# Second input tile sooner, later ones scaled by ScalarE; next MLP weights decoded mid-stage and split in the first half of stage four

## The reference, cut to what matters

```python
xn = layernorm(x)                                  # x: 8 x 256 tokens x 256
x  = x + attn(xn) + ffn(xn)
# attn, 16 heads of 128: q, k (with rope), v, g = xn @ W.T
#   s  = clip(xn @ Ws1.T @ Ws2.T + bs2, -32, 32)   # 64 slots a head
#   z  = cumlogsumexp(s); es = exp(s); enz = exp(-z)
#   A  = tril(q @ k.T) * scale
#   qv = softmax(enz * (A @ es))
#   o  = tril((qv * enz) @ es.T) @ v
#   out = (rmsnorm(o) * g_norm * silu(g)) @ Wo.T
# ffn: gate, up (2048 wide), down from 4-bit codes times scales per block of 32
#   out = (gelu(gate) * up) @ down.T
```

## Time and profile before

| | us |
|---|---|
| median of 3 runs | 1124.58 (1122.58 to 1124.82) |
| the profiled execution | 1122.49 |
| its span, first to last instruction | 1120.0 |
| TensorE busy | 1084.0 (97%) |
| VectorE busy | 928.1 (83%) |
| ScalarE busy | 650.6 (58%) |
| GpSimd busy | 425.5 (38%) |

### The profile page before, as it was taken

One profiled execution on the slowest core, in us unless ns is written; L12 is line 12 of the kernel. 1 busy time (PEld: TensorE's weight loads), 2 busy tenths in 40 slices (PEclk: granted clock), 3 DMA queues, 4 the chain that ended last, 5 costly groups with the idle time before them and its releaser, 6 DMA issues.

```text
span 1120.0 us, 20624 instructions
## 1 busy us (share of the span) xinstructions
PE 1084.0 (97%) x7176; PEld 927.7 (83%) x7176; DVE 928.1 (83%) x1687; ACT 650.6 (58%) x2103; POOL 425.5 (38%) x308
## 2 busy tenths in 40 slices
PE   6888999999999999999999999999999999999996
PEld 5677888888888888888888888888888888888875
DVE  6788889888888889888888888888888898888863
ACT  4465566655655657555666656565665556655542
POOL 7142245432524345232453324443252334523231
PEclk9899999999999999999999999999999999999996
DMA  4002000020002000020000200011000200000001
GB/s 166 1 1 78 1 2 1 2 77 1 1 1 78 1 2 1 1 78 1 1 1 1 78 1 2 1 38 41 1 1 1 78 1 1 1 1 20 1 20 38
DMA packets 9526, 23.06 MB, mean 21 GB/s; under 512 B 848, under 2 KB 5840, under 8 KB 8528
## 3 DMA queue, kind: packets, MB, share of 16 engines
q1 hardware_dynamic: 9424, 21.76, 5.4%
HBM read 19.66 MB, written 2.10 MB: 19 GB/s over the span
## 4 chain that ended last, share of the span: by engine, by line
PE 84%; DVE 7%; issue 4%; POOL 2%; ACT 2%; DMA 0%; POOLq 0%; DVEq 0%; ACTq 0%
PE bank L205 20%; PE bank L207 19%; PE bank L206 19%; PE bank L303 4%; PE bank L366 4%; PE bank L316 3%; PE bank L337 3%; DVE xs L930 2%; PE bank L375 2%; PE bank L305 2%; PE bank L328 1%; PE bank L529 1%; PE bank L346 1%; PE bank L319 1%; PE bank L359 1%
## 5 line engine op out<-in xcount | busy, mean ns | idle before, releaser
L1200 POOL TENSOR_TENSOR inter_lo<-ffb,inter_hi 128x512 fp32r<-128x512 f32 x64 | 83.3, 1325 | 440.5 <-ACT inter_hi L678 440.5
L1191 POOL TENSOR_TENSOR qkT<-ra,xs 128x512 f32<-128x512 f32 x128 | 170.2, 1329 | 109.6 <-DVE xs L930 80.8
L640 ACT ACTIVATE sm<-bank,mx 128x64 f32<-128x64 f32 x256 | 76.5, 326 | 120.6 <-DVE mx L886 120.6
L930 DVE TENSOR_TENSOR xs<-xs,rope 128x512 f32<-128x512 f32 x128 | 129.5, 1012 | 0.0
L927 DVE TENSOR_TENSOR ra<-bank,rope 128x512 f32<-128x512 f32 x128 | 87.7, 685 | 46.9 <-ACT xs L622 44.7
L621 ACT ACTIVATE xs<-bank 64x512 f32<-64x512 f32 x128 | 76.2, 595 | 66.8 <-PE bank L207 43.8
L205 PE MATMUL bank<-xh,wqk_hi 128*128 128x512 f32 x256 | 109.9, 429 | 3.1 <-DVE h L990 2.6
L875 DVE RECIPROCAL enzT<-enzT 128x256 f32<-128x256 f32 x64 | 111.4, 1742 | 0.0
L205 PE MATMUL bank<-xh,wgu_hi 128*128 128x512 f32 x256 | 105.6, 412 | 0.0
L645 ACT ACTIVATE At<-bank 128x128 f32<-128x128 f32 x128 | 35.8, 281 | 114.1 <-DVE At L809 112.9
L205 PE MATMUL bank<-wvg_hi,xh 128*128 128x512 f32 x256 | 101.1, 395 | 1.0 <-DVE xl L978 1.0
(11 more groups left out here) (149 smaller groups left out, 3075.5 us busy)
## 6 DMA issues: line engine op xcount, KB each, us to landing
raw<-in_w_qkvg SPq DMA_DIRECT2D x7, 1024.0 KB, 5.0
scaled<-in_w_scaled SPq DMA_DIRECT2D x8, 640.0 KB, 7.1
packed<-in_w_packed SPq DMA_DIRECT2D x8, 384.0 KB, 5.7
acc<-in_x SPq DMA_DIRECT2D x4, 512.0 KB, 8.1
out<-acc SPq DMA_DIRECT2D x3, 512.0 KB, 2.9
raw<-in_w_qkvg SPq DMA_DIRECT2D x2, 512.0 KB, 7.1
out<-acc SPq DMA_DIRECT2D x2, 256.0 KB, 2.1
ws_raw<-in_w_slot SPq DMA_DIRECT2D x8, 48.0 KB, 1.8
```

The lines of the kernel that those rows point to most:

```text
L640: ins = act.activation(sm[:, c], src[:, c], ACT.Exp, bias=mx[:, g:g + 1], accum_out=ssum[:, g:g + 1])
L930: dve.tensor_tensor(two(xs[i % 2][:, :]), two(xs[i % 2][:, :]), sin, ALU.mult).then_inc(sin_done, 1)
L1191: pool.tensor_tensor(qkT[:, i, :], ra[i % 2][:, :], xs[i % 2][:, :], ALU.add).then_inc(roped, 1)
L1200: pool.tensor_tensor(inter[1][e][:, :], ffb[e][:, :], inter[0][e][:, :].bitcast(F32), ALU.subtract).then_inc(inter_lo, 1)
```

## The change

SyncE: x 1 is loaded fourth, ahead of `ws1`, `packed`, `ws2_raw`, `scaled`; of the next head pair `packed` is loaded first. The layer norm has buffers of its own (`xvar`, `xrs`, `xnb`) in place of `mse` and `rstd`. x 2 and x 3 are no longer scaled by VectorE but by ScalarE, which needs a bias of -mean times scale that VectorE makes (`x_bias`). On the way in, VectorE does the statistics of x 1 at once, scales x 1 between the decode steps, and takes the first gates in between too; both transposes of x 1 follow each other; `slot_scores(None, 0, 0)` and `slot_inner(1)` stand ahead of stage 0, and the statistics of x 2 too. In stages 0 and 1 the first transposes of the next x come after `outputs` and `project_vg`.

For every head pair: `decode` of the next one runs in the middle of stage two (steps 0, 1) and three (steps 2, 3, 4); before, steps 1 and 3 stood at stage ends and step 4 in stage four. `prepare_scales` moves to stage three, `prepare_out` to stage one of its own head pair. In stage four the high and low parts of VG, QK and GU are all made before `softmax_exp`.

`wqk_hi` now stands between the two `off_diagonal` copies (At), where before it came after `copy_state`. The core of the diff:

```diff
@@ SyncE
             load_x(0)
...
+            load_x(1)
             sp.dma_start(ws1, w_slot1).then_inc(ws1_in, 16)
...
-            load_x(1)
@@ TensorE
             project_qk(0, 0, 0, 1)
             transpose_x(1, 0, rg[1])
+            transpose_x(1, 1, sc[0])
             project_qk(0, 0, 0, 2)
             project_qk(0, 0, 0, 3)
+            pe.wait_ge(h1_done, 2)
+            pe.wait_ge(h1_lo, 1)
+            slot_scores(None, 0, 0)
+            slot_inner(1, sc[1])
...
                 for i in (0, 1):
+                    if first and i == 1:
+                        pe.wait_ge(h1_done, 4)
+                        pe.wait_ge(h1_lo, 2)
...
+                if not first:
+                    outputs(st, 0, php, None)
+                if not last:
+                    project_vg(st + 1, nbp, nhp, 2, True)
                 if prep:
                     pe.wait_ge(clip_done, st + 2)
                     transpose_x(prep, 0, sc[0])
-                if not first:
-                    outputs(st, 0, php, None)
-                if not last:
-                    project_vg(st + 1, nbp, nhp, 2, True)
                 slot_rows(st)
@@ ScalarE
+            def x_scale_act(bp):
+                act.wait_ge(xnb_done, bp - 1)
+                if bp == 3:
+                    act.wait_ge(xT_full, KT * bp)
+                for i in range(NT):
+                    ins = act.activation(xn[bp][:, i, :], acc[:, bp * NT + i, :], ACT.Identity,
+                                         bias=xnb[:, i:i + 1], scale=xrs[:, i:i + 1])
+                ins.then_inc(xn_act, 1)
...
+                if bp == 0 and not first:
+                    prepare_out(hp)
+                if bp == 2 and more:
+                    prepare_scales(hp + 1)
                 if bp == 3 and more:
                     split_hi(hp + 1, W_VG)
                 off_diagonal(st, 2)
+                if bp == 3 and more:
+                    split_hi(hp + 1, W_QK)
                 off_diagonal(st, 3)
                 gate_square(st, 1)
+                if first:
+                    x_scale_act(prep)
...
                 copy_state(st)
+                if bp == 3 and more:
+                    split_hi(hp + 1, W_GU)
+                if st == 1:
+                    x_scale_act(prep)
@@ VectorE
+            def x_bias(bp):
+                dve.wait_ge(xpow_done, bp + 1)
+                wait(dve, xn_act, bp - 2)
+                dve.scalar_tensor_tensor(out=xnb[:, :], in0=mv[:, :, 0], scalar=-1.0, in1=xrs[:, :],
+                                         op0=ALU.mult, op1=ALU.mult).then_inc(xnb_done, 1)
...
+                softmax_in(st, par)
+                if first:
                     cumulate(1, 1)
-                softmax_in(st, par)
...
+                if bp == 2 and more:
+                    decode(hp + 1, 2)
+                    decode(hp + 1, 3)
                 softmax_max(st)
...
                     add_share(st, pbp, 0)
+                if bp == 1 and more:
+                    decode(hp + 1, 0)
+                    decode(hp + 1, 1)
                 if bp == 2 and more:
-                    decode(hp + 1, 2)
-                if bp == 3 and more:
                     decode(hp + 1, 4)
@@ GpSimd
                 if bp == 3 and more:
                     dequantise(hp + 1, W_GU)
+                    split_lo(hp + 1, W_GU)
...
                         rotate(st + 1, i)
-                        if i == 1 and bp == 3 and more:
-                            split_lo(hp + 1, W_GU)
```

More of the change, by code:

```diff
@@ L476, in stage @@
                 if first:
-                    pe.wait_ge(h1_done, 2)
-                    pe.wait_ge(h1_lo, 1)
-                    slot_scores(None, 0, 0)
                     mlp_up(st, bp, hp, 2)
-                    slot_inner(1, rg[1])
                 else:
@@ L757, in stage @@
                     x_hi(prep, 1, sc[0])
-                if bp == 3 and more:
-                    split_hi(hp + 1, W_QK)
-                    prepare_scales(hp + 1)
-                    prepare_out(hp + 1)
                 if last:
@@ L777, in stage @@
                     copy_J(st + 1, rg[1][:, :])
-                if bp == 3 and more:
-                    split_hi(hp + 1, W_GU)
                 if bp == 2 and more:
@@ L996, in _ @@
             x_lo(0, 1, rg[1])
-            for part in range(5):
-                decode(0, part)
+            x_stats(1)
+            decode(0, 0)
+            decode(0, 1)
+            x_scale(1)
+            gate_g(0, 0, 0)
+            gate_g(0, 0, 1)
+            decode(0, 2)
+            decode(0, 3)
+            decode(0, 4)
+            gate_g(0, 0, 2)
+            gate_g(0, 0, 3)
             slot_lo(0)
-            for i in range(NT):
-                gate_g(0, 0, i)
-            x_stats(1)
             dve.wait_ge(const_in, 32)
             dve.wait_ge(consts, 1)
+            inner_lo(0, rg[0])
             rope_cos(0, 0)
             rope_sin(0, 0)
-            x_scale(1)
             rope_cos(0, 1)
             rope_sin(0, 1)
-            inner_lo(0, rg[0])
             x_lo(1, 0, rg[1])
+            x_lo(1, 1, sc[0])
             rope_cos(0, 2)
             rope_sin(0, 2)
-            x_lo(1, 1, rg[1])
             rope_cos(0, 3)
             rope_sin(0, 3)
+            inner_lo(1, sc[1])
+            x_stats(2)
             def stage(hp, bp, first, last):
@@ L1033, in stage @@
                     gate_gelu(st, 0)
-                    inner_lo(1, rg[1])
                 else:
@@ L1092, in stage @@
                 slot_query(st, par)
-                if bp == 1 and more:
-                    decode(hp + 1, 0)
                 if not last:
@@ L1109, in stage @@
                     rope_sin(st + 1, 3)
-                if bp == 1 and more:
-                    decode(hp + 1, 1)
-                if bp == 2 and more:
-                    decode(hp + 1, 3)
             def last_gate(h):
@@ L1234, in _ @@
             dequantise(0, W_GU)
-            x_pow(1)
+            rotate(0, 0)
             split_lo(0, W_GU)
-            for i in range(4):
+            for i in range(1, 4):
                 rotate(0, i)
+            x_pow(2)
             def stage(hp, bp, first, last):
```

56 lines of the change are left out of this document (29 added, 27 removed).

## The result

The changed kernel ran in four timed executions: median 1111.19 us (1109.47 to 1113.46), against 1124.37 us for the kernel before beside it. The ratio is 0.9887, with a 95% interval of 0.9864 to 0.9910. The forecast was 1114.0 us (1110.0 to 1118.5). The profiled execution of after is its slowest one, 1113.46 us, with a span of 1110.7 us; before's was the fastest of its runs, 1122.49 us with a span of 1120.0 us. So the two profiles lie only 9.3 us apart in span, where the medians lie 13.2 us apart.

The account below looks back on a forecast made before the run. TensorE, busy 97% of the 1120.0 us span, was taken as the bound. 1122.49 - 6.5 - 0.1 + 0.6 - 3.5 = 1113.0 us for the profiled execution, carried to a forecast of 1114.0 us, range 1110.0 to 1118.5.

Parts of the forecast that it names:

- The way in: Start to stage 0's softmax transposes: the 6.35 us wait for the second x goes, smaller waits come; gain 6.5 us.
- the chain of four steps: New TensorE waits up to stage 0's softmax: slot_inner(1) 2.2, scores(1) 1.4, score_diagonal 0.4, x transposes 1.4 us.
- ScalarE's scaling: Stage 0: ScalarE scales x 2 in four activations, 0.36 to 0.4 each, 1.3 to 1.6 us, ahead of copy_J.
- Stage 1: Wait for scaled x goes, but two decode steps delay the third query/key projection: gain 0.1 us, idle there 2.8 us.
- The clock: TensorE's granted clock may fall after the new shorter waits: loss 0.6 us, bounds 0 and 3.
- The borders: Seven head-pair changes, each losing 0.5 us, mostly behind waits on qkT: gain 3.5 us, bounds 0 and 3.8.
- What was added for the median: Before's median lay 2.1 us above its profiled run; half carried over, from 1113.0 to 1114.0 us.
- Rival A: Way in gives back half through ScalarE's scaling, xl waits and a lower clock, also in stage 1: 1117.2 us; chance 0.17.
- step 4: Stage 0: ScalarE scales x 2, VectorE is relieved; gains slot_reads 3.4, slot_rows 6.9, softmax transposes 6.5 us.
- Rival B: Borders keep their 0.5 us because the third rotate is late for another reason (swap, A_full): 1117.5 us; chance 0.08.
- Rival C: Stage four: VectorE's two scans held beside GpSimd work reading SBUF, 2.4 us each; slower, about 1132 us; chance 0.04.
- Rival D: Better than forecast, no low clock anywhere in the way in: 1110.5 us; chance 0.07.

Follow-up runs that it names:

- after_again: The changed kernel itself, nothing altered, run again on another chip: 1111.95 us, ratio 0.9905 to the kernel before.
- scale_on_vector: The changed kernel with x 2 and x 3 scaled by VectorE again, without the bias, instead of by ScalarE: 1112.97 us, ratio 0.9909.
- the memset: The changed kernel plus a GpSimd memset (2.38 us, only writes) between second and third rotate at each head-pair border: 1110.95 us, ratio 0.9898.
- fill_subtract: The changed kernel plus a GpSimd subtraction (2.36 us, reads SBUF) between second and third rotate at each head-pair border: 1114.42 us, ratio 0.9922.
- x1_late: The changed kernel with the load of the second x back in eighth place instead of fourth: 1110.65 us, ratio 0.9892.

## Why the prediction was right, and where it was not

**The sum.** It was made against the profiled execution: -6.5, -0.1, +0.6, -3.5, which gives -9.5. The profile of after shows -9.3 of span, and its terms are these:

- The way in, 6.5: measured 7.2, of it 0.4 by the earlier load and 0.7 by ScalarE's scaling, as far as one profile each can tell. The place is right, and the chain of four steps is right in its order; TensorE waited 2.13, 1.04, 0.20 and 1.15 us at the four places where 2.2, 1.4, 0.4 and 1.4 stood. What was mis-sized is VectorE's part between x and its scaling: I let the long decode step and the scaling take turns with GpSimd as before, and had x scaled at 19.0 us. It was ready at 17.7, because `wqk_lo` ended as the step began (0.96 us instead of 3.04). The transposes came 1.2 us sooner than forecast, and what follows kept 1.0 to 1.2 of that until `slot_rows`; the fall of the clock at 50 to 54 took some back before the softmax (5.96 us from `slot_rows` to it in after, 5.57 in after_again).
- ScalarE's scaling, 1.3 to 1.6 us: it took 2.07, some 0.52 for one of 128x256. My upper bound of 0.4 for one was too low. TensorE's wait for `esJ` grew from 0.29 to 0.63 us; in scale_on_vector, without that work on ScalarE, it is 0.37.
- Stage 1, 0.1: measured +0.46 from softmax 0 to 1 and -0.8 from 1 to 2 (the clock apart), so a loss of some 0.35. The prediction let the two decode steps reach the third projection, and they do: it starts 7.71 us behind the softmax of stage 1, in before 6.93. The idle time ahead of it, 0.90 and 1.45 us, is 2.35 where 2.8 stood. From the start of the profile to that projection (100.71 against 107.56 us) 6.85 us were gained, with 6.6 forecast: that stage gave 0.4 less than forecast, and the way in 0.7 more.
- The clock, 0.6 with bounds 0 and 3: 1.54 us in stage 1, in five of the nine profiles with these two waits. That is 0.9 as a mean, so 0.6 was no bad middle, but no profile has it; the profiled one paid 1.54. What the falls ahead of that cost is inside the 7.2 and the 0.46 us.
- The borders, 3.5: measured 4.0. Six of before's borders cost 0.51, one 0.78, and the stage behind each 0.03: 4.0 in all.
- Together: 0.7 and 0.5 us more gain than forecast at the way in and the borders, 0.4 and 0.9 less in stage 1 and by the clock. That the profiled execution came out within 0.5 us of its forecast is in part luck, since the misses cancel.
- What was added for the median, +1.0: wrong, in sign as well. The profile of before was the fastest of its runs and I took half of its lead over to after; but after's own profile is its slowest, 2.3 us above its median. The term is off by 3.3 us, and that is more than the 2.8 between 1114.0 and 1111.19; the profiled execution itself was forecast at 1113.0 and came out at 1113.46. Two parts of it can be told from the sections: with the clock at 1.00 in stage 1, as in four of nine profiles, the same execution would have had 1.5 us less, and with the end of after_again 2.5 us less. The prediction had no term for the end; before's end took 25.62 us, as after's did, so between these two profiles it cancels; between the medians it need not. What the median execution of before contains more than its profile is still not seen: no second profile of before was taken.

**Rival A** (the way in gives back half) did not come: slot_rows and the softmax kept more than the 3.4 us of step 4. Its second leg did, though: the clock fell in stage 1, for 3.5 us (101.7 to 105.2), at 1.5 us. **Rival B** falls with the borders at 32.91 us: neither the swap nor A_full kept them at 33.4. Another reason that the prediction had not weighed, a rotate late by GpSimd's queue, is refuted by the memset. **Rival C** is real as a mechanism (a scan held for 0.36 us, the product for 1.9 in fill_subtract), and its times stayed in the slack, as the prediction had it: VectorE was idle for 1.85 us soon behind, at 292.11. **Rival D** gave 1110.5, and no profile of the changed kernel is without a fall in stages 0 and 1; two of its executions took 1109.47 and 1110.17 us all the same, at a mean granted clock of 0.993 and 0.991, where the two longer ones have 0.988; where in them the clock fell was not profiled.

**The change's own claim**, the second x sooner, is worth 0.4 us by the profiles; I had put the gain to the load and the order together, and only x1_late tells them apart. For the border, I argued with a row (the 2.58 us product) that a queue could have explained too; the two fillers tell them apart.

## What to carry to other kernels

When a step at a border is slow, ask first which engine's instruction stands beside it and from where both read: moving 2.4 us of GpSimd work that reads SBUF away from VectorE's two-operand products gave 4 us here, while the same length of work that only writes costs nothing in that place. Before a transfer is moved ahead, see whether the engine behind it is free to take it: here the earlier load gave 0.4 of 7.2 us, and the rearranged work the rest. And a distance to a median that one profile cannot show should not be carried over to another kernel with a sign: give it to the range.

## What the runs showed of the hardware

- A VectorE `tensor_scalar` on 128x4 numbers took 1.00 us instead of 0.17 when GpSimd's `wqk_lo` (2.40 us) ran beside it, and ended when that ended (14.59 and 14.56 us). It has one operand tile, so the hold is not only for two. The Trainium skill, page "SBUF — State Buffer", section "Who interferes with whom", lists `tensor_scalar` among the operations that can take the shared pair of ports. The two rows agree with that.
- TensorE's granted clock is not a property of the program: in the changed kernel, with the same waits (0.90 and 1.45 us), it fell to 0.50 for some 3.5 us in two profiles and stayed at 1.00 in the third. The price is the same each time: from softmax 1 to 2 38.58 to 38.60 us in four profiles, 37.04 to 37.06 in four others. In after_again it fell behind the 2.14 us wait at 28 us instead (0.60 and 0.54 in 28:30 and 30:32), which it did not in after; what chooses is not seen.
- ScalarE's scaling of 128x256 costs 0.52 us in a series of four (2.07 us), against 0.724 for 128x512.
